# A ring of 12 input tiles, a loop of TensorE that is entered in the middle of its body, and a last group stored in three column parts, in a kernel for packed lower triangles of Gram matrices

## The reference

```python
B, N, D = (1024, 64, 256)            # the input that is used has 2048 batches
Z = jnp.einsum('bnd,bmd->bnm', inputs, inputs)
li, lj = jnp.tril_indices(n, k=-1)
return Z[:, li, lj]
```

## Time and profile before

| | |
|---|---|
| Median of 3 runs | 398.13 us (397.13 to 398.52) |
| The profiled execution | 397.29 us, of it a span of 395.5 us from the first to the last instruction |
| Busy | TensorE 368.8, VectorE 370.4, ScalarE 188.3, GpSimd 200.3 us |
| DMA | 150.99 MB, on average 382 GB/s |
| Granted clock of TensorE | 0.5 of full speed (1.2 GHz) from 10 to 25 us, full speed (2.4 GHz) from 30 us on while it works |

### The profile page before, as it was taken

The page is one execution under the profiler, slowest core; times in us unless marked ns, Lnnn a source line. Parts: engine busy times, 40 slices in busy tenths (PEclk is TensorE's granted clock), DMA queues, the critical chain, the costliest instruction groups (busy, mean ns, idle before and its releaser), DMA issues.

```text
span 395.5 us, 69567 instructions
## 1 busy us (share of the span) xinstructions
PE 368.8 (93%) x33280; PEld 363.7 (92%) x33280; DVE 370.4 (94%) x369; ACT 188.3 (48%) x858; POOL 200.3 (51%) x975
## 2 busy tenths in 40 slices
PE   4389999999999999999999999999999999999960
PEld 4389999999999999999999999999999999999960
DVE  3258899999999999999999999999999999999995
ACT  0021245454545555555555455545554555545572
POOL 2000075482828456382837557282846648282765
PEclk9569999999999999999999999999999999999995
DMA  8999999999999999999999999999999999994307
GB/s 321 423 421 419 423 422 418 380 424 423 416 405 389 427 420 423 398 422 418 411 422 362 426 423 422 416 419 421 413 420 377 427 414 417 385 416 162 114 16 193
DMA packets 21274, 150.99 MB, mean 382 GB/s; under 512 B 2688, under 2 KB 2816, under 8 KB 4864
## 3 DMA queue, kind: packets, MB, share of 16 engines
q1 hardware_dynamic: 18912, 136.81, 85.5%
q10 hardware_dynamic: 2336, 13.94, 8.7%
HBM read 134.22 MB, written 16.52 MB: 381 GB/s over the span
## 4 chain that ended last, share of the span: by engine, by line
DVE 44%; issue 29%; PE 24%; ACT 0%; DVEq 0%; ACTq 0%
DVE x_turned L232 31%; PE bank_set L309 24%; DVE row_halves L249 11%; DVE x_in L256 1%; DVE packed_rows L154 1%; DVE packed_rows L143 0%; ACT packed_rows L143 0%; DVE x_turned L261 0%; DVEq L248 0%; ACT products L336 0%; DVEq L75 0%; DVEq L279 0%; ACTq L332 0%
## 5 line engine op out<-in xcount | busy, mean ns | idle before, releaser
L309 PE MATMUL bank_set<-x_turned 32*64 32x64 f32 x33280 | 368.8, 237 | 13.1 <-issue 11.1
L309 PEld LDWEIGHTS bank_set<-x_turned 32*64 32x64 f32 x33280 | 363.7, 131 | 18.0 <-issue 11.7
L232 DVE STREAM_TRANSPOSE x_turned<-x_in 128x1024 f32<-128x1024 f32 x256 | 295.7, 1207 | 19.3 <-PE bank_set L309 15.6
L154 POOL COPY packed_rows<-row_halves 32x32 f32<-32x32 f32 (+30 forms) x930 | 191.7, 206 | 187.5 <-DVE row_halves L249 149.9
L336 ACT COPY products<-bank_set 128x512 f32<-128x512 f32 x128 | 75.1, 586 | 146.6 <-PE bank_set L309 130.9
L249 DVE STREAM_TRANSPOSE row_halves<-products 128x1024 f32<-128x1024 f32 x60 | 72.2, 1203 | 0.0
L143 ACT COPY packed_rows<-row_halves 128x32 f32<-128x32 f32 (+30 forms) x465 | 61.2, 218 | 12.5 <-DVE row_halves L249 12.3
L149 ACT COPY packed_rows<-row_halves 128x128 f32<-128x128 f32 x240 | 54.1, 300 | 15.0 <-DVE row_halves L249 13.3
L336 ACT ACT_TABLE_LOAD x1 | 1.3, 1283 | 26.0 <-PE bank_set L309 26.0
L154 POOL COPY packed_rows<-x_in 32x32 f32<-32x32 f32 (+30 forms) x31 | 5.0, 212 | 2.2 <-DVE x_in L256 2.2
L256 DVE STREAM_TRANSPOSE x_in<-products 128x512 f32<-128x512 f32 (+1 forms) x5 | 4.6, 995 | 0.0
## 6 DMA issues: line engine op xcount, KB each, us to landing
x_in<-x_dram SPq DMA_DIRECT2D x128, 1024.0 KB, 15.1
y_dram<-packed_rows ACTq DMA_DIRECT2D x20, 504.0 KB, 8.9
y_dram<-packed_rows SPq DMA_DIRECT2D x4, 504.0 KB, 5.0
y_dram<-packed_rows ACTq DMA_DIRECT2D x6, 252.0 KB
y_dram<-packed_rows ACTq DMA_DIRECT2D x24, 63.0 KB
y_dram<-packed_rows SPq DMA_DIRECT2D x1, 380.0 KB
y_dram<-packed_rows ACTq DMA_DIRECT2D x1, 380.0 KB
y_dram<-packed_rows SPq DMA_DIRECT2D x1, 124.0 KB
```

The lines of the kernel that those rows point to most:

```text
L154: return copy(packed_rows[first:first + BLOCK, group % 2, :, at + BLOCK:at + i], halves(group)[first + BLOCK:first + HALF, i, :, 0:i - BLOCK])
L232: nc.vector.transpose(x_turned[:, j, chunks].rearrange("p c b s (h u n v) -> p u v (c b s h) n", h=ROWS // BLOCK, u=PAIRS, v=PAIR), x_in[: ...
L309: done = nc.tensor.matmul(bank_sets[j][side * HALF:(side + 1) * HALF, g, slot, :].rearrange("r (n u v) -> r u n v", u=PAIRS, v=PAIR), rows ...
```

## The change

- `IN_RING` goes from 11 to 12: one more slot for input tiles.
- `PARTIALS` goes from 2 to (1, 2): even tiles (buffer 0) are turned by one instruction of 128x2048 and handed over as a whole, odd tiles (buffer 1) as before in two halves. A turning of an even tile waits for the whole multiplication before it in that buffer.
- TensorE's loop body is now two blocks of code, "lap" (buffer 0) and "second" (buffer 1). The first branch goes to "second", so only one blank tile is multiplied in place of two, and buffer 0 needs no zeros.
- The last row turning of group 14 is done after tile 126, ahead of tile 127. ScalarE packs group 14 wholly by tile 126, waits for GpSimd's carries and stores one side of group 14 itself before it evicts tile 127.
- The last eviction is split into long rows (32 to 63) and short rows; run 1 of the last group is turned in two pieces of 128x1024 instead of four of 128x512.
- The last group is stored in three column parts (rows 48 to 63, rows 32 to 47, the short rows), on both sides. The short rows are packed by VectorE (1 to 10), GpSimd (11 to 15) and ScalarE (31 down to 16, with the issue of part 1 amid them).

```diff
-    IN_RING = 11
+    IN_RING = 12
     LAP = 2
+    PARTIALS = (1, 2)
...
-    PARTIALS = 2
-    PARTIAL = CHUNKS // PARTIALS
...
-    LAST_HOME = (GROUPS * PIECES - 2) * 4 + 2
+    BY_POOL = (11, 16)
+    LAST_PARTS = [slice(first_column(3 * ROWS // 4), PACKED), slice(first_column(BLOCK), first_column(3 * ROWS // 4)),
+                  slice(0, first_column(BLOCK))]
...
+        def laps_done(j, lap):
+            return lap - (1 if j == 0 else 0)
...
+        def wait_last_kept(engine, long):
+            lap, s = place(TILES - 1)
+            engine.wait_ge(kept[s], (lap + 2) * LAP - (1 if long else 0))
...
+        def store_last(engine, side, part):
+            group = GROUPS - 1
+            if part < LONG_PIECES:
+                engine.wait_ge(packed_home, group * PIECES + part + 1)
+                engine.wait_ge(packed_across, group * LONG_PIECES + part + 1)
+                engine.wait_ge(last_carried, part + 1)
+            else:
+                engine.wait_ge(last_packed, 3)
+            store(engine, group, LAST_PARTS[part], WHOLE_SIDES[side:side + 1])
...
-                    sync.wait_ge(turned[j][PARTIALS - 1], (lap + 1) * LAP)
+                    sync.wait_ge(turned[j][-1], (lap + 1) * LAP)
...
-                store(sync, group, slice(0, PACKED), WHOLE_SIDES)
-            store_last(sync, 0)
+                store(sync, group, slice(0, PACKED), WHOLE_SIDES if group < GROUPS - 2 else WHOLE_SIDES[0:1])
+            for part in range(len(LAST_PARTS)):
+                store_last(sync, 0, part)
...
-            for j in range(BLANK):
-                nc.gpsimd.memset(x_turned[:, j, PARTIAL:CHUNKS], 0.0).then_inc(turned[j][1], LAP)
+            pool.sem_inc(turned[0][0], LAP)
+            nc.gpsimd.memset(x_turned[:, 1, CHUNKS // 2:CHUNKS], 0.0).then_inc(turned[1][1], LAP)
...
-                for h in range(PARTIALS):
-                    chunks = slice(h * PARTIAL, (h + 1) * PARTIAL)
-                    dve.wait_ge(multiplied[j][h], lap)
+                for h in range(PARTIALS[j]):
+                    chunks = slice(chunks_of(j, h).start, chunks_of(j, h).stop)
+                    if laps_done(j, lap) > 0:
+                        dve.wait_ge(multiplied[j][h], laps_done(j, lap))
...
-            for n in range(turned_rows, (GROUPS - 1) * PIECES):
-                turn_rows(n)
...
+                if t == TILES - 2:
+
+                    for n in range(turned_rows, (GROUPS - 1) * PIECES):
+                        turn_rows(n)
...
-                    for piece in range(PIECES):
-                        turn_last_rows(run, piece_rows(piece)).then_inc(rows_turned, 1)
+            wait_last_kept(dve, True)
+            turn_last_rows(RUNS - 1, slice(BLOCK, ROWS)).then_inc(rows_turned, LONG_PIECES)
+            wait_last_kept(dve, False)
+            turn_last_rows(RUNS - 1, slice(0, BLOCK)).then_inc(rows_turned, PIECES - LONG_PIECES)
...
-            for i in range(1, piece_rows(PIECES - 1).stop):
+            for piece in range(LONG_PIECES):
+                rows = piece_rows(piece)
+                for i in range(max(BLOCK + 1, rows.start), rows.stop):
+                    last = carry_across(nc.vector.tensor_copy, GROUPS - 1, i, 1)
+                last.then_inc(last_carried, 1)
+            for i in range(1, BY_POOL[0]):
...
-            pe.br("lap")
+            pe.br("second")
             with nc.body("lap", valid_engines=[pe.engine]):
-                for j in range(LAP):
-                    multiply(j)
+                multiply(0)
+            with nc.body("second", valid_engines=[pe.engine]):
+                multiply(1)
                 pe.br_lt(count, (LAPS + 1) * LAP, on_true="lap", on_false="laps_done")
...
+                by_rows = (slice(0, ROWS),) if t < TILES - 1 else (slice(BLOCK, ROWS), slice(0, BLOCK))
...
-                while n + PACK_LAG < 2 * (t + 1):
+                end = 2 * (t + 1) - PACK_LAG
+                if t >= TILES - 3:
+
+                    end = (GROUPS - 1) * PIECES * 4 - 4 * max(0, TILES - 2 - t)
+                while n < end:
                     pack(n)
                     n += 1
-            for n in range(n, LAST_HOME):
+                if t == TILES - 2:
+                    act.wait_ge(packed_home, (GROUPS - 1) * PIECES)
+                    act.wait_ge(packed_across, (GROUPS - 1) * LONG_PIECES)
+                    store(act, GROUPS - 2, slice(0, PACKED), WHOLE_SIDES[1:2])
+            for n in range(n, ((GROUPS - 1) * PIECES + LONG_PIECES) * 4):
                 pack(n)
-            store_last(act, 1)
+            store_last(act, 1, 0)
+            act.wait_ge(rows_turned, GROUPS * PIECES)
+            for i in range(BLOCK - 1, BY_POOL[1] - 1, -1):
+                if i == BY_POOL[1] + 3:
+
+                    store_last(act, 1, 1)
+                last = pack_short(nc.scalar.copy, GROUPS - 1, i)
+            last.then_inc(last_packed, 1)
+            store_last(act, 1, 2)
```

More of the change, by code:

```diff
@@ L98, in gram_lower_triangle @@
         loaded = [semaphore(f"loaded{k}") for k in range(IN_RING)]
-        turned = [[semaphore(f"turned{j}_{h}") for h in range(PARTIALS)] for j in range(LAP)]
+        turned = [[semaphore(f"turned{j}_{h}") for h in range(PARTIALS[j])] for j in range(LAP)]
         kept = [semaphore(f"set_kept{s}") for s in range(SETS)]
-        multiplied = [[semaphore(f"multiplied{j}_{h}") for h in range(PARTIALS)] for j in range(LAP)]
+        multiplied = [[semaphore(f"multiplied{j}_{h}") for h in range(PARTIALS[j])] for j in range(LAP)]
         rows_turned = semaphore("rows_turned")
@@ L116, in place, with chunks_of @@
             return divmod(t + BLANK, LAP)
+        def chunks_of(j, h):
+            some = CHUNKS // PARTIALS[j]
+            return range(h * some, (h + 1) * some)
+        def laps_done(j, lap):
+            return lap - (1 if j == 0 else 0)
         def wait_kept(engine, t):
@@ L190, in _ @@
                 sync.wait_ge(packed_across, (group + 1) * LONG_PIECES)
-                store(sync, group, slice(0, PACKED), WHOLE_SIDES)
-            store_last(sync, 0)
+                store(sync, group, slice(0, PACKED), WHOLE_SIDES if group < GROUPS - 2 else WHOLE_SIDES[0:1])
+            for part in range(len(LAST_PARTS)):
+                store_last(sync, 0, part)
             for b in range(2):
-                last = 2 * len(WHOLE_SIDES) * 16 if (GROUPS - 1) % 2 == b else 0
+                last = len(LAST_PARTS) * len(WHOLE_SIDES) * 16 if (GROUPS - 1) % 2 == b else 0
                 sync.wait_ge(stored[b], stores_before(GROUPS + b) + last)
@@ L216, in _ @@
             pool.wait_ge(packed_across, GROUPS * LONG_PIECES)
-            pool.wait_ge(rows_turned, GROUPS * PIECES - 1)
-            rows = piece_rows(PIECES - 2)
-            for i in range(rows.start + PIECE // 2, rows.stop):
+            pool.wait_ge(rows_turned, GROUPS * PIECES)
+            for i in range(*BY_POOL):
                 last = pack_short(nc.gpsimd.tensor_copy, GROUPS - 1, i)
@@ L258, in turn_last_rows @@
                     products[:, (GROUPS - 1) % KEPT_RING, rows, run * BLOCK:(run + 1) * BLOCK])
-            for j in range(BLANK):
-                nc.vector.memset(x_turned[:, j, 0:PARTIAL], 0.0).then_inc(turned[j][0], LAP)
+            nc.vector.memset(x_turned[:, 1, 0:CHUNKS // 2], 0.0).then_inc(turned[1][0], LAP)
             turned_rows = 0
@@ L267, in _ @@
                     turned_rows += 1
-            for n in range(turned_rows, (GROUPS - 1) * PIECES):
-                turn_rows(n)
-            for run in range(RUNS):
+                if t == TILES - 2:
+                    for n in range(turned_rows, (GROUPS - 1) * PIECES):
+                        turn_rows(n)
+            for run in range(RUNS - 1):
                 wait_kept(dve, (GROUPS - 1) * GROUP_TILES + (run + 1) * GROUP_TILES // RUNS - 1)
-                if run < RUNS - 1:
-                    turn_last_rows(run, slice(0, ROWS))
-                else:
-                    for piece in range(PIECES):
-                        turn_last_rows(run, piece_rows(piece)).then_inc(rows_turned, 1)
+                turn_last_rows(run, slice(0, ROWS))
+            wait_last_kept(dve, True)
+            turn_last_rows(RUNS - 1, slice(BLOCK, ROWS)).then_inc(rows_turned, LONG_PIECES)
+            wait_last_kept(dve, False)
+            turn_last_rows(RUNS - 1, slice(0, BLOCK)).then_inc(rows_turned, PIECES - LONG_PIECES)
             wait_packed_free(dve, GROUPS - 1)
             dve.wait_ge(rows_turned, GROUPS * PIECES)
-            for i in range(BLOCK + 1, ROWS):
-                last = carry_across(nc.vector.tensor_copy, GROUPS - 1, i, 1)
-            last.then_inc(last_carried, 1)
-            for i in range(1, piece_rows(PIECES - 1).stop):
+            for piece in range(LONG_PIECES):
[4 more added lines that the diff above has]
+            for i in range(1, BY_POOL[0]):
                 last = pack_short(nc.vector.tensor_copy, GROUPS - 1, i)
@@ L292, in multiply @@
             def multiply(j):
```

(15 more changed lines are left out.)

2 lines of the change are left out of this document (1 added, 1 removed).

## The result

The changed kernel takes 391.49 us (median of 5 runs, 391.17 to 392.56) against 397.77 for the kernel before, measured beside it: a ratio of 0.9843, 95% interval 0.9829 to 0.9857, so 1.6% faster. The profiled execution took 391.2 us, its span 389.3.

The account below looks back on a forecast made before the run. VectorE was taken to bound from 61 us on, with TensorE and DMA close behind; DMA would cut the gain at tile 120. Gains 3.2 + 0.1 + 0.5 + 0.4 = 4.2 us gave 394.0 us, range 391.6 to 397.0.

Parts of the forecast that it names:

- The entry amid the body: TensorE's start: jumping to "second" halves the blank work, ending it at 16.7 to 19.3 us, 2.1 to 4.7 sooner.
- the cheaper bound: TensorE's start: if each hole costs 3.8 us, as between bursts, the blank part ends at 16.7 us.
- Rival (a): Loop's jump back: TensorE fetches the first two code blocks again, 7.6 us more, time 398.5 to 401.1; chance 0.11.
- no DMA engine starves: Ring of 12: DMA is full throughout, so earlier issue leaves landing times unchanged; value 0, bounds 0 to -1 us.
- the sum of 4.2: Whole kernel's gain: 3.2 us at tile 120, 0.1 turnings, 0.5 packs and 0.4 final stores.
- rival (c): Loads: landings come sooner than forecast (12 slots, stores elsewhere), span 388.3, time 390.9 us; chance 0.08.
- (d): Laps: whole-tile handover costs more than the 0.3 us spare, TensorE waits each lap, time 400 us; chance 0.05.
- The cut: Tile 120: its load lands at 354.1 us, so VectorE starts it at 354.2 instead of 357.4, gaining only 3.2.
- The whole even tile: Laps: VectorE's lap falls from 5.63 to 5.58 us, so TensorE's 5.594 sets it; 2 us up to tile 120.
- The end: After VectorE starts tile 120: turnings gain 0.1 us, short packs 0.5, final stores 0.4.
- chain of 34.2 us from tile 120: Forecast time from TensorE taking up tile 120 to the end: 16.8 + 5.6 to its last matmul, then 11.8.
- The cover of the moved store: Group 14's store on ScalarE: its wait for GpSimd's carries stays hidden, carries 378.7, eviction 379.6, 0.6 us cover after issue.

Follow-up runs that it names:

- e6b_at_lap_split: The changed kernel entered at "lap" with two blank tiles, buffer 0's zeros written in halves by VectorE and GpSimd: 396.55 us, ratio 0.9965.
- e3_entry: The kernel before with only the loop entered at "second" and one blank tile; 11 slots, halves and old end kept: 393.40 us, ratio 0.9891.
- e10_ring9: The changed kernel with IN_RING = 9 instead of 12: 394.09 us, ratio 0.9895.
- e7_halves: The changed kernel with PARTIALS = (2, 2), both tiles in halves again: 392.55 us, ratio 0.9854.
- e4_whole: The kernel before with PARTIALS = (1, 2) and its whole-tile handover, still entered at "lap": 398.16 us, ratio 1.0013.
- e5_old_end: The changed kernel with the end of the kernel before (last row turning, eviction, packs and stores): 391.85 us, ratio 0.9853.

## Why the prediction was right in sign and wrong in size

- **The entry amid the body: right.** Three waits for code, the burst sizes and the 16.7 us of the cheaper bound are what the trace shows. Undone by itself (e6b_at_lap_split) it is worth 5.4 us, alone in the kernel before (e3_entry) 4.2. Rival (a), code fetched a second time, did not come: there are 4 packets and no hole in the laps. The Trainium skill's rule (Runtime: NRT & Kernel Launch, Instruction fetch mechanics) holds for the jump ahead, which waited from 0.9 to 5.1 us; the first jump back, from the last block to the first, took from 16.65 to 16.89 us, as long as before the change, so there the trace does not agree with a window of two pages.
- **The step that failed: "no DMA engine starves ... landing times stay, because loads and 13 groups of stores before them are the same bytes".** The bytes are the same, the rate is not. At an equal share of 1.01 the DMA moves 414 GB/s with a short queue and 421 with a long one, and the last load lands at 371.5 or at 368.3. The page showed it already before the change, in the line under the share: of its 40 slices of GB/s some stand at 362 to 389 amid many at 420 to 427. With a landing at 351.0 instead of 354.1 nothing was cut at tile 120. VectorE took it at 352.4, 5.0 us sooner than before (357.4), where the sum has 354.2 and 3.2: 1.8 of the 2.0 us missing from the sum of 4.2. So rival (c) came, with 0.08 the least likely but (d). It named 12 slots as a cause, and these are only a part of it: the earlier start lengthens the queue as well, and 10 and 11 slots give the same time. Its sum of 388.3 us for the span is 1.0 short of the 389.3 measured, mostly by TensorE's laps (5.604 where it had 5.594, 0.6 us over 58).
- **The cut itself is real, only its place was off.** With 9 slots the same kernel waits for loads and loses 3 us (e10_ring9). With 10 to 11, VectorE takes tile 120 within 0.1 us of its landing. The changed kernel stands 0.9 to 1.4 us from this edge.
- **The whole even tile: a small term, mis-sized in the laps.** TensorE's lap was forecast at 5.594; it was 5.604 in the first profile and 5.593 in the second, and the ends are the same (389.3 and 389.2), as the second began 0.9 us later. From tile 4 to tile 120 it took 325.0 us before and after: VectorE's slower laps before the change had been hidden by its lead, up to 278 us (tile 90), and cost 0.6 us up to tile 120. The changed kernel lost as much in that profile, by a lap of 5.604 all the way. Undone (e7_halves) it is worth 1.35 us, some 0.8 to 0.9 of it from tile 120 on.
- **The end: right in the sum that was taken, 1.2 us for 1.0.** Counted as the sum counts, from VectorE's start of tile 120: the turnings took 28.4 us where they took 28.3 before (0.1 lost where 0.1 was to be gained), the copies behind them 0.6 less (0.5 forecast), the final stores 0.6 less (0.4). These are the other 0.2 of the missing 2.0.
- **The same 6.2 us counted at TensorE** are 4.4 at tile 120's eviction and 1.8 behind it. From that eviction to the end: 33.2 us before, 32.4 to 32.5 with whole tiles alone (e4_whole, e5_old_end), 32.2 with the new end alone (e7_halves), 31.3 to 31.4 with both. So the new end is worth 1.0 to 1.1, and the other 0.7 to 0.8 are VectorE no longer being behind TensorE. The forecast had this in its chain of 34.2 us from tile 120 (36.1 before).
- **The cover of the moved store** held: GpSimd's carries ended at 376.7, the store went out at 376.9, the last eviction began at 377.9.
- The three engines did end together, at 385.5 to 386.0 us, against 387.2 to 387.3 forecast.

Not settled: what inside the DMA makes more of the load packets slow when few loads are queued; why the length of a code fetch's hole differs between 3.6 and 4.8 us from execution to execution, which moves the whole kernel by up to 1 us; and why TensorE's laps average 5.593 to 5.598 us in some executions, 5.604 in the first profile of the changed kernel, evenly, and 5.605 to 5.609 in three others through a few long ones.

## What to carry to other kernels

Beside a full DMA share, read the GB/s of the same slices: a share says busy, not fast, and a landing time is not fixed by the bytes alone. When the step before a bound is made faster, ask whether it also lengthens the queue in front of that bound, and test the bound by making the queue shorter until the time gives way. Where an experiment undoes a part, look at its first microseconds before its time: a memset twice as long let TensorE begin 1.1 us later in two runs here, as much as the effects that were asked for.

## What the runs showed of the hardware

- TensorE's code of 16 KB blocks (256 instructions) is fetched on first use with holes of 3.6 to 4.8 us each while the DMA is full of loads. A jump ahead into a block not yet fetched cost one such wait (4.2 us; 3.9 to 4.4 in the other runs), and the blocks passed over stayed available for the jump back (0.24 us, still 4 packets).
- DMA throughput of the loads with stores between them depended on the number of loads queued: 411 GB/s with the shortest issue-to-landing at 4.8 us, 419 at 10.6, 420 to 421 from 12.6 us on, always at a busy share of 1.00 to 1.01. The loss lies in a few load packets of over 0.4 us, where the median is 0.31: 286 in the kernel before, 103 in the changed one.
